# A graph attention network with a routed expert layer on one core: one of every 64 gathered chunks moved from GpSimd to SyncE, tile numbers turned on TensorE, expert results in two halves

## What is computed

```python
h = (x @ W).reshape(n, heads, -1)            # 4 heads of 64, then 1 head of 256
e = leaky_relu(al_s[src] + al_d[dst], 0.2)   # al_s, al_d: h times two attention vectors
ex = exp(e - m[dst])                         # m: the segment's maximum
alpha = ex / (segment_sum(ex, dst) + 1e-16)
out = segment_sum(h[src] * alpha, dst) + b   # self loops are added to the edges
...
x = x + gnn(layernorm(x))
x = x + sum over top-2 experts of p * (gelu(ln(x) @ w1 + b1) @ w2 + b2)
```

## Time and profile before

| | us |
|---|---|
| median of 3 runs | 5240.36 (5238.65 to 5241.19) |
| the profiled execution, its own time | 5236.12 |
| its span | 5234.5 |
| start phase and first shift | 0 to 160 |
| edge phase of layer 1 | 160 to 2200 |
| projection and second shift | 2200 to 2315 |
| edge phase of layer 2 | 2315 to 4356 |
| mid x, gate, routing, scatter | 4356 to 4687 |
| experts | 4687 to 5212 |
| combine | 5212 to 5234.5 |

### The profile page before, as it was taken

One profiled execution on the slowest core, in us unless ns is written; L12 is line 12 of the kernel. 1 busy time (PEld: TensorE's weight loads), 2 busy tenths in 40 slices (PEclk: granted clock), 3 DMA queues, 4 the chain that ended last, 5 costly groups with the idle time before them and its releaser, 6 DMA issues. The chain is left out here.

```text
span 5234.5 us, 76220 instructions
## 1 busy us (share of the span) xinstructions
PE 3631.5 (69%) x12542; PEld 2230.4 (43%) x12543; DVE 3422.5 (65%) x8917; ACT 1488.3 (28%) x3315; POOL 3424.8 (65%) x3626
## 2 busy tenths in 40 slices
PE   5477777777777777757777777777777774219996
PEld 4244444444444444434444444444444443206664
DVE  5677777777777777776777777777766776504442
ACT  3222222222222222342222222222222222103232
POOL 4577777777777777537777777777777772353332
PEclk8677777777777878777777777777777776559998
DMA  5344444444444444325555555555555555123334
GB/s 138 108 132 132 133 133 132 133 133 134 133 133 132 133 133 133 94 90 139 138 138 139 138 138 139 139 139 139 139 138 138 139 136 162 69 79 56 55 56 87
DMA packets 298785, 644.90 MB, mean 123 GB/s; under 512 B 74539, under 2 KB 132779, under 8 KB 298322
## 3 DMA queue, kind: packets, MB, share of 16 engines
q0 software_dynamic: 183376, 475.89, 34.8%
q1 hardware_dynamic: 106882, 156.45, 10.8%
q10 hardware_dynamic: 8480, 12.06, 0.7%
HBM read 583.32 MB, written 68.80 MB: 125 GB/s over the span
## 5 line engine op out<-in xcount | busy, mean ns | idle before, releaser
L999 POOL DMA_INDIRECT rows<-table,idx x3232 | 3055.9, 946 | 1025.7 <-issue 919.8
L1072 PE MATMUL bank<-rows,hit 128*128 128x260 f32 (+1 forms) x6464 | 2620.7, 549 | 1080.7 <-DVE acc L1134 1065.3
L1072 PEld LDWEIGHTS bank<-rows,hit 128*128 128x128 f32 x6464 | 1467.1, 256 | 2031.7 <-DVE acc L1134 1778.2
L1134 DVE TENSOR_TENSOR acc<-acc,bank 128x260 f32 (+1 forms) x3232 | 1356.0, 420 | 180.4 <-issue 34.9
L1125 DVE TENSOR_TENSOR rows<-rows,bank 128x1024 f32<-128x1024 f32 x808 | 946.3, 1212 | 1.3 <-ACT rows L1032 1.3
L1029 ACT ACTIVATE arg<-arg 128x32 f32<-128x32 f32 (+1 forms) x404 | 88.4, 219 | 2833.7 <-DVE arg L1118 2833.7
L1111 DVE TENSOR_TENSOR arg<-rows,bank 128x32 f32<-128x32 f32 (+1 forms) x404 | 71.6, 177 | 999.9 <-DMA rows<-table,idx 999.9
L1092 DVE TENSOR_TENSOR hit<-bank,dst_loc 128x256 f32<-128x256 f32 x1616 | 672.9, 417 | 0.1
L1023 ACT ACTIVATE hit_t<-gap,ones 128x1024 bf16<-128x1024 bf16 x404 | 464.0, 1148 | 20.7
L1018 ACT ACTIVATE gap<-loc,minus_node 128x1024 bf16<-128x1024 bf16 x404 | 462.6, 1145 | 10.2 <-DMA loc<-loc_row 6.3
L1061 PE MATMUL bank<-du,hit_t 128*128 x3232 | 375.1, 184 | 119.6 <-ACT hit_t L1023 80.0
(11 more groups left out here) (200 smaller groups left out, 1976.8 us busy)
## 6 DMA issues: line engine op xcount, KB each, us to landing
loc<-loc_row SPq DMA_DIRECT2D x404, 256.0 KB, 3.5
rows<-table,idx POOLq DMA_INDIRECT x3232
sent<-zeros SPq DMA_DIRECT2D x202, 68.5 KB
xe<-sent SPq DMA_DIRECT2D x106, 129.0 KB, 2.0
fw<-in_L_ffn_W ACTq DMA_DIRECT2D x16, 512.0 KB, 10.6
table<-acc POOLq DMA_DIRECT2D x49, 130.0 KB
table<-acc POOLq DMA_DIRECT2D x49, 128.5 KB, 2.4
back<-mid_tile POOLq DMA_DIRECT2D x49, 128.0 KB, 2.1
```

What stands on the lines that cost most here:

```text
L999: pool.indirect_dma_start(rows[:, way, n, 0:R], None, table, bass.IndirectOffsetOnAxis(idx[:, way, n:n + 1], 0)).then_inc(rows_in[way], 16)
L1072: nc.tensor.matmul(sum_bank[n % 4][:, 0:R], hit[:, way, n, :], rows[:, way, n, 0:R], start=True, stop=True).then_inc(summed, 1)
L1134: nc.vector.tensor_tensor(kp.acc[:, t, 0:R], kp.acc[:, t, 0:R], sum_bank[n % 4][:, 0:R], ALU.add).then_inc(added, 1)
```

## The change

Edge phases: the loops of all engines run 8 steps in a turn (`TURN`). Of every 64 items the last (item 7 of step 7) is not gathered by POOL. SP fetches it: in ways 4 to 7 of a turn it loads 32 indices into registers after that step's `loc`, and issues 32 DMAs of one row each into `sp_rows`. ACT copies the attention terms of these rows (`copy_sp_term`) between `hit_t` and `weigh` of its step 6; DVE's `make_arg` of step 7 waits for that, and `scale_rows` reads the item from `sp_rows`. `src_row` is a new DRAM tensor with the source numbers of each item.

```diff
+    BATCH = 32
+    TURN = 2 * SETS
+    BY_SP = (TURN - 1, ST - 1)
...
+                def gather_rows(quarter):
+                    sp.load(regs, sp_idx[0:1, quarter * BATCH:(quarter + 1) * BATCH])
+                    for m in range(BATCH):
+                        n = quarter * BATCH + m
+                        row = sp.snap(regs[m], min_val=0, max_val=N - 1)
+                        sp.dma_start(sp_rows[n:n + 1, 0:R], table[bass.ds(row, 1), :]).then_inc(sp_rows_in[n // 64], 16)
+
+                def step(s, way, turn):
+
+                    fetches = not number(turn) or turn < STEPS // TURN
+                    if way == 4 and fetches:
+                        sp.wait_ge(sp_idx_in, (turn + 1) * 16)
+                    load(s, way, turn)
+                    if way >= 4 and fetches:
+                        gather_rows(way - 4)
+                    if way == 7 and (not number(turn) or turn + 1 < STEPS // TURN):
+                        load_idx(turn + 1)
...
                     for n in range(ST):
-                        pool.indirect_dma_start(rows[:, way, n, 0:R], None, table,
...
+                        if (way, n) == BY_SP:
+                            continue
+                        pool.indirect_dma_start(rows[:, way % SETS, n, 0:R], None, table,
...
+                def copy_sp_term(s, turn):
+
+                    for half in range(2):
+                        act.wait_ge(sp_rows_in[half], (turn + 1) * (16 * 64))
+                    act.wait_ge(summed, (s - SETS + 1) * ST)
+                    nc.scalar.copy(rows[:, SETS - 1, BY_SP[1], D:D + H], sp_rows[:, D:D + H]).then_inc(sp_term, 1)
...
+                        if way == BY_SP[0]:
+                            dve.wait_ge(sp_term, turn + 1)
```

```diff
+                    done.then_wait(tt(less[:, :, :], key[:, :].unsqueeze(1).to_broadcast([P, NT, NT]),
+                                      key[:, :].unsqueeze(2).to_broadcast([P, NT, NT]), ALU.is_lt))
+                    done.then_wait(nc.vector.tensor_reduce(rank[:, :], less[:, :, :], AX.X, ALU.add))
+                    done.then_wait(tt(less[:, :, :], less[:, :, :],
+                                      length[:, :].unsqueeze(1).to_broadcast([P, NT, NT]), ALU.mult))
+                    done.then_wait(nc.vector.tensor_reduce(begin[:, :], less[:, :, :], AX.X, ALU.add))
...
+                    if t == ITEMS_AT + 5:
+                        sp.wait_ge(tile_kept, 1)
+                        sp.dma_start(kp.tile_row[:, :], tile_i[:, :]).then_inc(tile_written, 16)
```

```diff
-                    if not number(k) or k >= 1:
-                        pool.wait_ge(y_out[1 - way % 2], (turn * (RING // 2) + (way + 1) // 2) * 16)
-                        pool.reg_add(due, due, 0)
                     pool.indirect_dma_start(kp.back, bass.IndirectOffsetOnAxis(home[:, way:way + 1], 0),
-                                            ye[:, way % 2, :], None, compute_op=ALU.add).then_inc(y_out[way % 2], 16)
+                                            ye[:, way % 2, :], None).then_inc(y_out[way % 2], 16)
...
-                sp.dma_start(out[:, :], kp.back[SLOT_TILES * P:SLOT_TILES * P + N, :]).then_inc(stored, 16)
+                    for a in range(2):
+                        sp.dma_start(got[0:few(t), j, a, :], kp.back[bass.ds((t + a * NT + SLOT_TILES) * P, few(t)), :]).then_inc(got_in[j], 16)
...
+                    nc.scalar.activation(got[0:few(t), j, 1, :], got[0:few(t), j, 1, :], ACT.Copy,
+                                         scale=fb.pick[0:few(t), t, 1:2]).then_inc(weighed, 1)
...
+                    nc.vector.scalar_tensor_tensor(m, got[0:few(t), j, 0, :], fb.pick[0:few(t), t, 0:1], m, ALU.mult, ALU.add
+                                                   ).then_inc(added, 1)
+                    dve.wait_ge(weighed, t + 1)
+                    dve.wait_ge(added, t + 1)
+                    nc.vector.tensor_tensor(m, m, got[0:few(t), j, 1, :], ALU.add).then_inc(ready, 1)
```

More of the change, by code:

```diff
@@ L335, in _ @@
                                  pad[0:1, W - rest:]).then_inc(windows_written, 16)
-                sp.wait_ge(xt_zeroed, 1)
-                for t in range(SETS):
-                    load(t)
                 sp.wait_ge(windows_written, 8 * 16)
@@ L940, in edge_phase @@
         arg = b.sb(f"arg_{layer}", [P, 2, ST, H], F32)
+        sp_idx = b.sb(f"sp_idx_{layer}", [1, P], I32)
+        sp_rows = b.sb(f"sp_rows_{layer}", [P, D + HEADS], F32)
+        sp_idx_in = b.sem(f"sp_idx_in_{layer}")
+        sp_rows_in = [b.sem(f"sp_rows_in{half}_{layer}") for half in range(2)]
+        sp_term = b.sem(f"sp_term_copied_{layer}")
         idx_ready = b.sem(f"idx_ready_{layer}")
@@ L969, in _ @@
                     sp.wait_ge(zeros_ready, 2)
+                regs = [sp.alloc_register(f"sp_row{m}_{layer}") for m in range(BATCH)]
                 def load(s, way, turn):
@@ L1007, in stage @@
                 def stage(s, way, turn):
+                    half = way // SETS
+                    way = way % SETS
                     if not number(s) or s >= SETS:
-                        act.wait_ge(rows_in[way], turn * (16 * ST))
+                        act.wait_ge(rows_in[way], gathered(way, half, turn))
                     nc.scalar.copy(idx[:, way, :], eb.src_idx[:, bass.ds(s * ST, ST), 0]).then_inc(idx_ready, 1)
@@ L1046, in _ @@
                 weigh(0, 0)
-                steps(act, STEPS, step, SETS)
+                steps(act, STEPS, step, TURN)
             @block.tensor
@@ L1141, in step @@
                     nxt, later = (way + 1) % SETS, (way + 2) % SETS
+                    by, after = (way + 1) % TURN, turn + (way + 1) // TURN
                     if follows:
@@ L1158, in step @@
                         if ahead:
-                            make_arg(s + 1, nxt, turn + (way + 1) // SETS, stage)
+                            make_arg(s + 1, by, after, stage)
                         if follows:
@@ L1560, in load, with load_both @@
                         sp.wait_ge(home_ready, k - 1)
-                        sp.wait_ge(share_ready, k - 1)
                     sp.dma_start(xe[:, j, :], kp.sent[bass.ds(k * P, P), :]).then_inc(x_in[j], 16)
-                steps(sp, T, load)
+                def load_both(t, j, pair):
+                    load(t, j, pair)
+                    sp.dma_start(kp.acc[:, t, 0:D], kp.mid[bass.ds(t * P, P), :]).then_inc(mid_in, 16)
+                steps(sp, NT, load_both)
+                load(NT, NT % 2, NT // 2)
+                with sp.Fori((NT + 1) // 2, T // 2) as pair:
+                    for j in range(2):
+                        load(pair * 2 + j, j, pair)
+                sp.wait_ge(mid_in, 16 * NT)
             @block.gpsimd
@@ L1697, in step @@
                 def step(k, way, turn):
-                    j, pair = way % 2, turn * (RING // 2) + way // 2
+                    j, pair = way % 2, turn * 2 + way // 2
                     if not number(k) or k + 1 < T:
@@ L1720, in gelu, with step @@
                     nc.scalar.activation(hid[:, j, :], hid[:, j, :], ACT.Gelu).then_inc(gelu_ready, 1)
[L1722 to L1726 removed]
                 copy_x(0, 0)
                 copy_x(1, 1)
[L1731 to L1732 removed]
+                def step(k, j, pair):
+                    gelu(k, j)
                     if not number(k) or k + 2 < T:
[L1734 to L1739 removed]
+                        copy_x(k + 2, j)
+                steps(act, T, step)
 def combine_phase(nc, kp, fb, out):
@@ L1745, in combine_phase @@
         b = kp.within(ctx)
+        SETS = 7
+        got = b.sb("got", [P, SETS, 2, D], F32)
+        got_in = [b.sem(f"got_in{j}") for j in range(SETS)]
+        weighed = b.sem("second_weighed")
+        added = b.sem("first_added")
+        ready = b.sem("out_ready")
         stored = b.sem("out_stored")
+        few = lambda t: LAST if number(t) and t == NT - 1 else P
+        at = lambda t, rows: slice(t * P, t * P + rows) if number(t) else bass.ds(t * P, P)
         with nc.Block() as block:
```

247 lines of the change are left out of this document (158 added, 89 removed).

## The result

| | before | changed |
|---|---|---|
| median, us | 5240.77 (4 runs, 5238.65 to 5244.25) | 5579.59 (4 runs, 5574.58 to 5580.76) |
| ratio | | 1.0646, 95% interval 1.0630 to 1.0662 |
| the profiled execution, its own time | 5236.12 | 5580.16 |

The changed kernel is slower by 339 us. The forecast was 5730 in a range of 5210 to 5900: the direction held, and in the edge phases the mechanism too. The loss there was 104 us smaller than forecast, and the experts gained 70 us, for which I had zero.

The account below looks back on a forecast made before the run. POOL's descriptor writing was taken to bound the edge phases, four fifths of the time. 5236.1 + 452 (edge phases) + 6 (start) + 38 (combine with the end of the experts) = 5732, so 5730 us, range 5210 to 5900.

Parts of the forecast that it names:

- POOL paces before: Edge phases: POOL's descriptor writing sets the pace, a gather every 1.25 us, 80.0 us for eight steps.
- The chain: Edge phases: SP's fetches delay the next `loc`, making a turn 88.1 us in layer 1 and 90.0 in layer 2.
- A fetch: Edge phases, SP: one row fetch takes 0.48 us, 0.19 register work plus 0.29 DMA, bounded between 0.45 and 0.54.
- The register load: Edge phases, SP: loading 32 registers takes 1.6 us on a line, or 0.59 if flat.
- The sum of the edge phases: Both edge phases: 25 turns losing 8.1 us in layer 1 and 10.0 in layer 2, +452 us.
- Start phase: Before the first gather: -18 removed, +21 added on DVE, +3 for new waits, +6 us (-4 to +12).
- Experts: Experts stage: PE's 4.75 us a tile stays; removing `weigh_y` and the serial stores is worth nothing inside.
- Combine: Combine stage: 12.8 MB in and 6.4 MB out take 64 us, between 55 and 70, so +42 us.
- POOL keeps the pace: Edge phases rival: a fetch of at most 0.41 us lets SP's chain fit in 78.75 us; 5218 us, chance 0.20.
- the second rival: Edge phases: chain a little over the pace, fetch 0.41 to 0.45, turn 80 to 84 us, 5280 to 5500; chance 0.12.
- Fetches that queue on each other: Edge phases rival: queueing makes a fetch 0.62 us, time 6640, or 6120 at 0.54; chance of over 0.51: 0.14.
- POOL stalling on `idx`: Edge phases rival: fetches in time, but POOL stalls on `idx` staged by delayed ACT; within the forecast, no own chance.

Follow-up runs that it names:

- e12: Change with four `loc` buffers, `loc` two steps ahead, fetches in six parts cut at multiples of four, combine's second halves on ACT's queue: 5154.91 us, ratio 0.9842.
- e1: Change with only the row fetch undone, POOL gathering all 64 items again: 6490.93 us against 6501.26 for the kernel before on that chip, ratio 0.9979.
- e4: Change with ACT's operation put back into the experts as a multiplication by one, stores still plain: 7850.69 us against 6501.26 for the kernel before.
- e9: Change with ACT's multiplication by one put back into the experts, second run: 7784.10 us against 6378.55 for the kernel before on that chip.
- e10: Change with four `loc` buffers, `loc` two steps ahead, fetches in six parts of 22 or 21, clearing DMAs moved: 5611.72 us, ratio 1.0706.
- e11: Change with four `loc` buffers, `loc` two steps ahead, six fetch parts cut at multiples of four: 7571.78 us against 6372.76 for the kernel before, ratio 1.1862.
- e5: Change with four `loc` buffers instead of two and an earlier start of the fetches: 5303.44 us against 5240.75 for the kernel before, ratio 1.0118.
- e2: Change with four `loc` buffers and an earlier start of the fetches, first run: 7590.19 us against 6501.26 for the kernel before, ratio 1.1677.

## Why the prediction was right in its mechanism, and where its steps were off

- **POOL paces before: right.** e12 shows it from the other side: take one gather in 64 away without a late chain, and a turn goes from 80.0 to 78.8 us.
- **The chain, step by step.** Forecast for layer 1: 70.9 us from T0 to the next turn's `loc`, 3.5 to land, 13.6 behind it, 88.1. Measured in one turn: T0 is 613.1 (the end of ACT's `gap` of step 2 and SP's release), so 68.9 to the issue at 682.0, 3.9 to land, and 13.5 behind it to the next T0 at 699.4, in all 86.3. The tail of 13.6 was nearly exact. ACT's wait was 17 us for the forecast 14.
- **A fetch: mis-sized.** 0.418 us instead of 0.48, below the 0.45 I had given as the bound. Its DMA takes 0.227 us where the shortest static load of the earlier trace rows took 0.262, and its register work, one fused operation and a move, 0.19 as forecast (0.418 - 0.227). The bound was wrong because it took the nearest DMAs for a floor: -7.9 us a turn.
- **The register load: mis-sized the other way.** 2.06 us instead of 1.6 in layer 1, +2 us a turn; in layer 2 a median of 2.38 (2.18 to 2.98), +3 us a turn, for a reason that I didn't follow. The line from one to eight registers in the earlier trace rows doesn't go on as a line.
- **The branch: missed.** 2.4 to 3.2 us of SP without an instruction (median 2.5) behind each of the 44 branches back to the head of the long loop, and 0.35 us three times on the way; the prediction had no term for it. The long loop has 420 SP instructions in a turn. With 11 in a turn, the kernel before, the same gap is 0.12 us; with 27, e1 without the fetches, it is 0.12 us too, though e1 ran on the slower kind of chip. So the gap comes with the length of the loop. The Trainium skill (Runtime: NRT & Kernel Launch, "Instruction fetch mechanics") says that a taken branch outside the window already loaded stops the engine until its page is fetched; the trace agrees: a packet of instructions starts inside the gap shown above (at 680.20). The page of the profile counts such packets without naming their engine: 34 before, 288 in e1, 549 in the changed kernel.

```profile
q14 instruction: 549, 4.50, 0.2%
```

- **The sum of the edge phases: +348 instead of +452.** A turn lost 6.0 + 9.6 = 15.6 us instead of 18.1, which over 25 turns is 62 us of the difference. The other 42 is in the number of turns (132.7 / 6.0 and 215.2 / 9.6 are both about 22): POOL's lead covers the first, and behind the last fetches no next turn waits, so some 22 turns lose in each layer, not 25. That a turn came out within 2 us of the forecast is partly luck: the fetch took 7.9 us off, the register loads and the branch with its 0.35 us gaps, which was not in the sum, put 5.5 back. The measured fetch alone in my sum would have given 5732 - 6400 x 0.062 = 5335 us.
- **Start phase: +13.0 instead of +6.** DVE's busy time rose by 20.8 us (99.5 to 120.3; forecast 21) and its waits for x fell by 20.1 (26.4 to 6.3; forecast 18). What I left out are DVE's other waits, 12 us longer: 5.2 for ACT's root, 2.9 at the end of the block, 2.1 for the gathered windows and some small ones. The 3 us I gave for all that was the mis-sized term. In the runs that share this start phase the first gather came between 169 and 175 us, so a few us of the 13 are scatter.
- **Experts: the step that failed.** "ACT's `weigh_y` and the serial stores ran beside it, so their removal is worth nothing inside" is false: together they were worth 70 us. `weigh_y` alone holds the 507 us (e4, e9), and the stores, by the estimate above, would have held 492. ACT was 30% busy, and I took that for cover. But the earlier trace rows had PE busy 93.52 of 100, and the 6.48 missing had an owner: they were the ring. The busy share even understated it: 6.48% of 507 is 33 us, while the count of matmuls in 100 us went from 381 to 439, 15% more, which fits the 70 us. Where PE paces, its rate of instructions says more than its busy share.
- **Combine: nearly right.** +46.9 from the last matmul on against +38, of which combine itself is 70.6 - 22.5 = +48 for the forecast +42. I had taken 64 between 55 and 70, and the upper end was the right one. The end of the experts, for which I had -4.5 us, gave 1.4: from the last matmul to combine's first DMA 13.0 us instead of 14.4.
- **The rivals.** POOL keeps the pace would have needed a fetch of at most 0.41 us; the fetch was 0.418, and with the load and the branch the chain was 7 to 11 us over. By the size of the fetch alone the kernel belonged to the second rival (0.41 to 0.45), by its turn of 86.0 and 89.6 us to the forecast: I had tied the cases to one term, and two others moved. Fetches that queue on each other did not occur (0.224 to 0.308 us for each of the 6400). POOL stalling on `idx` was a small part: 95.9 us against 424.6 for PE's sums, and the fetches did not come out in time.
- **The two rules with another outcome.** The Trainium skill (Runtime: NRT & Kernel Launch, "Instruction fetch mechanics") gives 200 ns for each register of a load: not so for loads that begin at a multiple of four numbers (2.1 us for 32), and so for the others, where 4.67 us for 22 is 212 ns each. The Trainium skill (DMA: Bandwidth & Descriptors, "Issuing engines are not separate DMA queues") has issuing on several engines save issue time alone, as a rule a small matter. Issue time is indeed what was saved, 1.25 us for each gather moved, but here it is the whole pace: the DMA share of the edge phases was 0.51 and 0.54 even in e12, and a turn went from 80.0 to 78.8 us once the order on SP was right.

What stays open: which of e12's edits on SP's queue are needed, the four buffers, the earlier start, `loc` ahead or the six steps (only the cuts of the list were changed by themselves, from e10 to e12); how much of the 70 us each of the two removals in the experts is worth by itself; and what the start phase would give back if the ranking of the tiles were left out (not tried).

## What to carry to other kernels

When work is moved to an idle engine, its length is not what counts but what stands behind it in that engine's queue: the same 128 fetches a turn cost 348 us in front of a load that another engine waited for, and gave back 61 us when that load stood ahead of them and the register loads were short. An engine's low busy share is no cover either: look for the shares that are missing on the engine that paces, and ask which short operation on another engine lies in the ring. And cut lists of numbers for register loads at multiples of four: with the load ahead but badly cut lists (e10) the kernel was no faster than the change.

## What the runs showed of the hardware that I had not expected

- A register load costs by where it begins. From a multiple of four numbers: 1.39 us for 20, 1.6 for 24, 2.06 for 32 (2.38 in layer 2 of the changed kernel). From elsewhere: 4.46 us for 21 and 4.67 for 22. SP's six loads of a turn took 21.5 us in e10 and 8.8 in e12.
- A single-row DMA with an address from a register takes SP 0.227 us, and 0.418 us from one to the next with its register work, beside POOL's gathers every 1.25 us.
- A branch back to the head of a loop of 420 instructions cost SP 2.5 us, to that of one of 11 or 27 instructions 0.12.
- On some chips the same program runs with longer pauses between instructions. The same edge phases in e11 and in e12, 24 fetches and the next ones in SP's queue:

```profile
699.67 25.96 SPq L1068 DMA_DIRECT2D sp_rows<-table  x24
...
728.39 25.19 SPq L1068 DMA_DIRECT2D sp_rows<-table  x24
```

```profile
573.63 9.99 SPq L1068 DMA_DIRECT2D sp_rows<-table  x24
...
586.38 9.87 SPq L1068 DMA_DIRECT2D sp_rows<-table  x24
```

In e11 some stretches ran with pauses of up to 0.7 us between one instruction of SP and the next, others (20 fetches in 8.23 us) at full speed; POOL's gathers kept their 946 ns. The kernels with fetches suffered most, by 43 to 47% (e5 against e2, e12 but for its edit in combine against e11), the kernel before by 22 to 24%. Why these chips do so, I can't say; the supply of instructions would fit the pattern, and was not tested.
